# Scores of the global queries made once instead of twice in the second attention of a transformer pair on one Trainium2 core

## What is computed

```python
local_ok = (rel <= 0) & (rel >= -(lw - 1))          # lw = 128
key_global = (k_idx % gs == 0)[None, :]             # gs = 64
query_is_global = (q_idx % gs == 0)[:, None]
allowed = (local_ok | key_global | query_is_global) & (rel <= 0)
scores = jnp.where(allowed, scores, jnp.float32(-1000000000.0))
w = jax.nn.softmax(scores, axis=-1)
out = jnp.einsum('bhtk,bhkd->bhtd', w, v)
```

## Time and profile before

| | us |
|---|---|
| median of 3 executions | 3097.73 |
| lowest, highest | 3094.49, 3100.23 |
| the profiled execution, as timed | 3095.59 |
| its span, first to last instruction | 3093.9 |

### The profile page before, as it was taken

The page is one execution under the profiler, slowest core; times in us unless marked ns, Lnnn a source line. Parts: engine busy times, 40 slices in busy tenths (PEclk is TensorE's granted clock), DMA queues, the critical chain, the costliest instruction groups (busy, mean ns, idle before and its releaser), DMA issues. The chain is left out here.

```text
span 3093.9 us, 105510 instructions
## 1 busy us (share of the span) xinstructions
PE 2944.3 (95%) x41228; PEld 2156.1 (70%) x41260; DVE 2622.5 (85%) x5413; ACT 1699.0 (55%) x3301; POOL 1270.7 (41%) x1570
## 2 busy tenths in 40 slices
PE   7999999999999899999996996999999979999998
PEld 4556777777777477777774654877777757777776
DVE  5778999999999599999994996777777679999997
ACT  5646887778787633333332773666565633333333
POOL 3561112112121244444441784565555644444442
PEclk9998999999999999999998997999999989999999
DMA  6682444444443222222222667555555332222221
GB/s 210 224 244 56 97 105 98 98 100 101 100 105 81 67 80 86 88 85 88 85 80 77 206 213 200 129 144 140 140 140 144 104 90 83 89 85 89 85 88 52
DMA packets 362151, 353.88 MB, mean 114 GB/s; under 512 B 79066, under 2 KB 298714, under 8 KB 361642
## 3 DMA queue, kind: packets, MB, share of 16 engines
q1 hardware_dynamic: 357162, 347.56, 41.2%
q10 hardware_dynamic: 4608, 0.79, 0.1%
HBM read 211.37 MB, written 135.27 MB: 112 GB/s over the span
## 5 line engine op out<-in xcount | busy, mean ns | idle before, releaser
L947 DVE TENSOR_REDUCE aA_nmax<-bank 128x1 f32<-128x512 f32 (+3 forms) x1216 | 714.6, 656 | 59.1 <-PE bank L1009 52.6
L991 ACT ACTIVATE aA_prob<-bank 128x512 f32<-128x512 f32 (+1 forms) x1216 | 617.5, 581 | 155.7 <-PE bank L1009 150.5
L1009 PE MATMUL bank<-aA_qk 96*32 96x512 bf16 (+17 forms) x12288 | 654.8, 317 | 15.8 <-issue 10.3
L1009 PEld LDWEIGHTS bank<-aA_qk 99*32 99x32 bf16 (+1 forms) x12288 | 407.8, 96 | 181.2 <-issue 51.4
L932 POOL TENSOR_SCALAR_AFFINE_SELECT aA_prob<-aA_prob 128x512 f32<-128x512 f32 x256 | 160.9, 634 | 666.9 <-ACT aA_prob L991 666.9
L1009 PE MATMUL bank<-aA_prob,aA_vq 128*32 128x512 f32 (+3 forms) x3072 | 356.3, 489 | 0.9 <-POOL aA_prob L932 0.9
L1499 PE MATMUL bank<-aB_qk 96*32 96x160 bf16 (+4 forms) x9344 | 311.9, 232 | 26.5 <-DVE aB_nfar L1378 15.0
L1499 PEld LDWEIGHTS bank<-aB_qk 96*32 96x32 bf16 (+3 forms) x9344 | 244.0, 99 | 110.4 <-issue 32.9
L1470 ACT ACTIVATE aB_prob<-bank 128x512 f32<-128x512 f32 (+1 forms) x512 | 262.4, 574 | 84.4 <-PE bank L1499 80.3
L1372 DVE TENSOR_REDUCE aB_nnear<-bank 128x3 f32<-128x480 f32 (+1 forms) x352 | 207.8, 636 | 55.2 <-PE bank L1499 50.4
L1353 POOL TENSOR_SCALAR_AFFINE_SELECT aB_prob<-aB_prob 128x512 f32<-128x512 f32 x256 | 163.4, 638 | 197.7 <-ACT aB_prob L1470 195.8
(11 more groups left out here) (211 smaller groups left out, 6288.7 us busy)
## 6 DMA issues: line engine op xcount, KB each, us to landing
aA_qk<-parts_A SPq DMA_DIRECT2D x384, 128.0 KB, 4.0
aB_qk<-parts_B SPq DMA_DIRECT2D x384, 128.0 KB, 3.3
parts_A<-pA_part SPq DMA_DIRECT2D x96, 256.0 KB, 4.8
parts_B<-pB_part SPq DMA_DIRECT2D x96, 256.0 KB, 3.0
o_A<-aA_o_sb SPq DMA_DIRECT2D x32, 512.0 KB, 2.9
o_B<-aB_o_sb SPq DMA_DIRECT2D x32, 512.0 KB, 2.9
pA_xin<-x SPq DMA_DIRECT2D x16, 512.0 KB, 4.5
v_A<-pA_vs SPq DMA_DIRECT2D x16, 512.0 KB, 4.6
```

The lines of the kernel that those rows point to most:

```text
L947: nc.vector.tensor_reduce(dst, src, AX.X, ALU.max, negate=True).then_inc(s["m_taken"], 1)
L991: nc.scalar.activation(dst, src, ACT.Exp, scale=SCALE).then_inc(s["e_taken"], 1)
L1009: return nc.tensor.matmul(out, lhsT, rhs, start=start, stop=True, skip_group_check=True)
```

## The change

The gmax units on line m are gone. PE makes the global queries' scores once, in the gexp units, whose two banks on line e are now read twice: by DVE for the maxima, then by ACT for the exponentials. The DVE task gmax waits for gexp of PE, counts on a semaphore of its own (`g_halves`), and frees no bank; ACT's gexp frees it, as before. The waits for loads and for `aB_qg` move from the gmax function to the gexp function. The due times are other ones, so that `plan` makes other lists.

```diff
         for c in range(2):
-            unit("m", "gmax", c, 180, "dve", 690 + 760 * c, -0.85, ("pool", "qg", n, 0))
+            put("pe", "gexp", c, 180, -0.8, ("pool", "qg", n, 0), line="e")
+            put("dve", "gmax", c, 690 + 760 * c, -1.5, ("pe", "gexp", n, c))
         for c in range(2):
-            unit("e", "gexp", c, 180, "act", 710, -0.7, ("dve", "gmax", n, 1), then=[("act", "gturn", pre, 0)])
+            put("act", "gexp", c, 710, -1.5, ("pe", "gexp", n, c), ("dve", "gmax", n, 1), ("act", "gturn", pre, 0), line="e")
...
         def global_maxima(n, c):
             p = n % 2
-            dve.wait_ge(s["m_made"], after("m", "gmax", n, c))
-            nc.vector.tensor_reduce(gmax[p][:, c:c + 1], bank_of("m", "gmax", n, c), AX.X, ALU.max,
-                                    negate=True).then_inc(s["m_taken"], 1)
+            dve.wait_ge(s["e_made"], after("e", "gexp", n, c))
+            nc.vector.tensor_reduce(gmax[p][:, c:c + 1], bank_of("e", "gexp", n, c), AX.X, ALU.max,
+                                    negate=True).then_inc(s["g_halves"], 1)
             if c == 1:
-                dve.wait_ge(s["m_taken"], after("m", "gmax", n, 1))
+                dve.wait_ge(s["g_halves"], 2 * n + 2)
...
-        def global_maxima(n, c):
+        def global_exp(n, c):
             if n < RING:
                 pe.wait_ge(fixed_loaded[n], 32)
             if n == 0:
                 pe.wait_ge(s["gfix_loaded"], 32)
             pe.wait_ge(qk_loaded[n % RING], qk_uses(n))
             pe.wait_ge(s["qg_made"], n + 1)
-            need(pe, s["m_taken"], bank_clear("m", "gmax", n, c))
-            global_scores(bank_of("m", "gmax", n, c), n, c).then_inc(s["m_made"], 1)
-
-        def global_exp(n, c):
             need(pe, s["e_taken"], bank_clear("e", "gexp", n, c))
```

More of the change, by code:

```diff
@@ L1197, in attend_sparse_stage @@
         "far_done", "pv_done", "out_done", "o_ready", "den_loaded", "rden_ready", "rden_stored",
-        "fold_done", "gfix_loaded", "qg_made", "vd_made", "vq_made", "vd_set", "g_least", "g_max")}
+        "fold_done", "gfix_loaded", "qg_made", "vd_made", "vq_made", "vd_set", "g_halves", "g_least", "g_max")}
     qk_loaded = core.sems(f"{name[0]}_qk_loaded", RING)
@@ L1642, in pv @@
             ins.then_inc(s["pv_done"], 1)
-        pieces = {"near": near_unit, "far": far_unit, "turn": turn_max, "gmax": global_maxima, "gexp": global_exp,
+        pieces = {"near": near_unit, "far": far_unit, "turn": turn_max, "gexp": global_exp,
                   "gturn": global_turn, "og": global_out, "exp": exp_unit, "fpv": far_pv, "pv": pv}
```

## The result

| | before | after |
|---|---|---|
| median, us | 3098.00 (3094.49 to 3100.23, 4 executions) | 3127.99 (3124.68 to 3130.70, 4) |
| the profiled execution, its span | 3095.59, 3093.9 | 3129.48, 3127.8 |

The change makes the kernel slower, by a ratio of 1.010 (95% interval 1.0087 to 1.0112), 30 us. I forecast 3106.5 with a range up to 3122: the sign was right, the size was not.

The account below looks back on a forecast made before the run. PE was taken to bound the stage. New waits less the saved pairs gave +0.76 us a cycle, less 0.45 of supply stalls returned: +0.31 over 28 cycles, +9 us, so 3106.5 us, range 3090 to 3122.

Parts of the forecast that it names:

- What bounds the kernel: Sparse attention stage: it runs at PE's pace, with 17.2 us a cycle when PE hardly waits.
- the walk behind an odd turn: PE's order after an odd turn: near 2 ends at 5.9 us, gexp starts at 5.4, new waits 1.6 us.
- Fold: End of an odd cycle: turn waits 0.2 us more for DVE's near 9, near 10 and fold, between 0 and 0.4.
- Gexp 0: Behind even turns: 0.3 us of wait for exp 6 and gexp 0 behind a late ACT, between 0 and 0.8.
- Supply stalls: PE standing inside units without a named releaser: 0.65 us a cycle before, 0.2 kept, so 0.45 returned.
- The middle in sum: The 28 full cycles between the first three and the last: +0.31 us each, +9 us.
- The first three and the last cycles I count at 0: Start and end of the stage: no change, since they wait for loads and for ACT, 2 us either way.
- the removed time comes off (1): Rival for PE's removed pairs: the whole 0.44 us a cycle stays saved, -14 us, 3083.6; chance 0.17.
- ACT's sequencer (3): Rival: rows' three DMAs mostly take 2.88 us, gexp starts later than about 5.7, +18 to +30 us; chance 0.12.
- a clock that falls (4): Rival: repeated 1 us waits bring PE's clock to 0.92 throughout, some 45 us more, 3143; chance 0.03.

Follow-up runs that it names:

- a_short: The changed kernel, with DVE's gmax reduction cut to 8 of each bank's 512 columns: 3134.76 us, ratio 1.0118.
- a_sp_short: The changed kernel, with rows' DMAs (heads 2 to 31) issued by SP instead of ACT and DVE's gmax reduced over 8 columns: 3133.32 us, ratio 1.0126.
- a_fold: The changed kernel, with POOL's clear 7 of an even head waiting for fold of the head two further: 3128.59 us, ratio 1.0099.
- b_thin_short: The kernel before, with gmax matmuls of 8 columns instead of 512 and DVE reducing only those 8: 3100.32 us, ratio 1.0001.
- a_ends: The changed kernel, with gexp 0 of head 0 planned behind near 3 and gexp 0 of the last head behind exp 13: 3118.92 us, ratio 1.0081.
- b_thin: The kernel before, in its own order, with gmax matmuls of 8 columns instead of 512: 3095.62 us, ratio 1.0005.
- a_twice: The changed kernel, with every gexp unit's four matmuls done twice into the same bank: 3128.33 us, ratio 1.0106.
- b_lay: The kernel before, with DVE's lay moved behind the far of three heads further: 3111.57 us, ratio 1.0036.
- a_late: The changed kernel, with the DMAs of rows moved on ACT's list behind the copy of gturn: 3158.04 us, ratio 1.0202.

## Why the prediction missed

- **What bounds the kernel** (PE, 17.2 us without waits) held, and so did the walk behind an odd turn, gexp's start at 5.4 included (5.44 on average). Near 2, exp 8 and exp 9 wait (0.95 - 0.29) + (0.63 - 0.14) + (0.26 - 0.14) = 1.27 us, forecast 1.6 between 1.0 and 2.1. That near 2 waits for DVE and gexp for ACT's DMA issues is what a_short and a_sp_short show.
- **Fold** was the mis-sized wait: 0.2 forecast, 0.4 at most, 1.04 - 0.26 = 0.78 measured. I took its 0.22 us from before, where from head 3 on it never stood beside one of POOL's clears; 0.44 of the surplus is that, as a_fold shows.
- **Gexp 0** I let wait 0.3 us behind even turns only. It waits behind both, (0.80 - 0.33) + (0.72 - 0.33) = 0.86: on line e it needs a bank that ACT empties, on line m gmax did not.
- **Supply stalls**: two cycles without waits should be 34.4 - 0.88 = 33.5 us; with 1.27 + 0.78 + 0.86 = 2.9 it is 36.4, and 36.57 was measured. So by this estimate 0.15 of these stalls were left where I kept 0.4; with 0.50 and 0.56 us for the pairs it is 0.3. That they shrink when PE waits anyway was right of PE's own (12.2 to 1.8 us) and wrong of the weight loads' (39.1 and 39.5); b_thin_short shows the other side, both grow when little else makes PE wait.
- The middle in sum: +13.1 us against +9. This alone would have been inside the range.
- **The step that failed**: "The first three and the last cycles I count at 0". They cost 8.2 + 7.2, and 1.7 behind them. I looked at what they wait for, not at where the new order puts the units in them: PE without near 2 and 3 in head 0, and gexp ahead of exp 8 to 13 in the last head, where ACT has the rows to issue first. And I priced gturn and og at full clock. The plans of both ends were there to be read beside the order that I did read. a_ends shows the end. Of the start, gturn and og of head 0 are 3.3 us, and 5.8 of the 8.2 are there by turn of head 0; which edit would have given them back is not shown.
- **Rivals.** That the removed time comes off (1) is out: b_thin and a_twice put the pair at 0 to 0.23 us. ACT's sequencer (3) was named with the right place and is half of the truth in the middle. That the measured 30 us lie at the edge of its range is chance: its condition didn't come (the three DMAs took 2.40 us on average behind odd turns, not 2.88, and gexp started at 5.44), and half of the 30 us are at the ends. As for the rest, a clock that falls (4) doesn't occur in the middle of the changed kernel, but in eleven of the variants it does.

## What to carry to other kernels

A saving on the engine that is full isn't worth what the removed work takes in the trace: 14 us by its starts, and 0 to 3 us when it was thinned or doubled. So measure one removed and one doubled before building on it. Where three engines' chains meet within a microsecond, cutting one moves the wait to the next, and here two cuts gave their microsecond back through the loads. Price the first and the last rounds of a pipelined schedule from the new order itself, at the clock that holds there.

## What I had not expected of the hardware

- Fold (DVE, two operands in SBUF) took 0.66 us in 14 heads, from right behind the start of POOL's instruction of 0.63 us until 0.06 us behind its end, and 0.22 us in 17 of the 18 others (head 2: 0.30); with POOL held back it took 0.22 in all but head 2. The page SBUF — State Buffer of the Trainium skill says under Who interferes with whom that a DVE instruction with two SBUF inputs contends with a GpSimd instruction that reads SBUF, and calls the pair of ports that they share an exclusive lock. The trace agrees, and a_fold is its test. I had looked up the price of fold, and not what it would stand beside.
- Matmuls of 8 columns instead of 512 (b_thin) saved 0.34 us of a pair's 0.50, and the next unit took 0.26 us more.
- In the middle of the variants TensorE's clock fell from its upper level (2.4 GHz) to its lower (1.2 GHz) 35 times, for 3.4 to 13.7 us. Ahead of 30 of these falls PE had stood once for 1.0 to 3.2 us, 1.04 us in a_fold, 3.23 in b_lay; but ahead of two in a_late it had stood for no more than 0.31 us at a time. And waits as long passed without a fall: 1.15 us in the earlier trace rows, 1.26 in the changed kernel, 1.87 in b_thin_short, 2.44 in a_sp_short. So one long wait goes with most falls and doesn't decide them; what does is not shown.
